# A mixing and scan kernel: preparation by whole chunks, with a third input buffer, a two-bank eviction and another order of the work

## The reference, cut to what matters

```python
# x: (16, 64, 128, 64) float32 = b, h, n, c;   4 heads, channel c = v * 4 + s
xg = group_norm(x)                                   # 32 groups of 2 channels, over h and n
mixed = einsum('mns,bwnvs->bwmvs', softmax(...), xg) # a 128 x 128 matrix for each head s
x = x + mixed + token_bias                           # called x1 below
y = group_norm(x)
row = y[:, 0]
for h in 1..63:  row = y[:, h] + relu(conv1d(row, W))   # 9 taps over n, 64 -> 64 channels
out = x + stack(rows)
```

## Time and profile before

| | |
|---|---|
| median of 3 runs | 876.46 us (875.48 to 876.52) |
| the profiled execution | 875.68 us, span 873.6 us |
| busy PE, DVE, ACT, POOL | 799.9, 618.7, 642.9, 435.7 us |
| preparation alone | from 24.4 to 236.1 us |
| scan with preparation | from 236.1 to 596.6 us |
| end of that wave, scan alone | to 604.0, to 873.6 us |

### The profile page before, as it was taken

How to read it: one execution, slowest core, us unless ns; L and a number is a source line. 1 busy time by engine, 2 the same in 40 slices (tenths; PEclk the granted TensorE clock), 3 DMA queues, 4 the chain that set the end, 5 groups by cost and what they waited for, 6 DMA issues and landing times.

```text
span 873.6 us, 20141 instructions
## 1 busy us (share of the span) xinstructions
PE 799.9 (92%) x5734; PEld 732.1 (84%) x5734; DVE 618.7 (71%) x1536; ACT 642.9 (74%) x1462; POOL 435.7 (50%) x416
## 2 busy tenths in 40 slices
PE   1778887888799999999999999997999999999997
PEld 1555555555599999999899999997999999999997
DVE  7677778777578888989797978765555555555553
ACT  2477777777758887888788888887677677677664
POOL 1665655566265655566566665662333333333333
PEclk9999999999999999999999999999999999999999
DMA  9334343433134444444434343221222222223223
GB/s 186 68 74 96 74 96 72 90 78 83 38 74 93 90 97 98 98 90 94 90 84 91 87 96 74 49 50 37 62 62 67 66 60 67 65 60 68 64 60 72
DMA packets 203159, 68.18 MB, mean 78 GB/s; under 512 B 137556, under 2 KB 203092, under 8 KB 203092
## 3 DMA queue, kind: packets, MB, share of 16 engines
q1 hardware_dynamic: 203092, 67.43, 35.0%
HBM read 33.85 MB, written 33.55 MB: 77 GB/s over the span
## 4 chain that ended last, share of the span: by engine, by line
PE 71%; issue 9%; ACT 7%; DVE 7%; POOL 3%; ACTq 1%; DMA 1%; SPq 1%; DVEq 0%; POOLq 0%
PE ps_conv L898 30%; PE ps_conv L902 15%; PE ps_mix L812 8%; PE ps_mix L814 6%; PE ps_out L890 5%; ACT x_paired L424 5%; PE ps_in L827 5%; PE ps_small L801 2%; POOL xs L341 2%; POOL total L364 1%; DVE carry L732 1%; DVE x_sb L642 1%; DVE st L553 1%; DVE st L649 1%; DMA x_sb<-in_x_dram 1%
## 5 line engine op out<-in xcount | busy, mean ns | idle before, releaser
L364 POOL TENSOR_TENSOR total<-x_paired,carry 128x256 f32<-128x256 f32 x256 | 193.5, 757 | 299.6 <-DVE carry L732 293.5
L341 POOL TENSOR_TENSOR xs<-x_sb,rstd 128x512 f32<-128x512 f32 x128 | 232.9, 1846 | 93.6 <-DVE rstd L624 66.8
L424 ACT ACTIVATE x_paired<-ps_in,shift 64x256 f32 (+1 forms) x512 | 237.9, 465 | 7.8 <-POOL total L364 1.2
L740 DVE TENSOR_TENSOR carry_l<-carry,carry_h 128x256 fp32r<-128x256 f32 x252 | 177.0, 703 | 86.3 <-ACT carry_h L483 83.7
L898 PE MATMUL ps_conv<-carry_h,wh 128*128 128x256 f32 x1280 | 219.7, 303 | 4.7 <-ACT carry_h L483 4.7
L463 ACT ACTIVATE rows<-x_paired,shift,rstd 128x128 f32 (+1 forms) x512 | 221.3, 481 | 0.9 <-DVE shift L672 0.7
L483 ACT ACTIVATE carry_h<-carry 128x256 fp32r<-128x256 f32 x252 | 105.8, 420 | 140.9 <-DVE carry L732 139.0
L898 PE MATMUL ps_conv<-carry_h,wl 128*128 128x256 f32 x1280 | 197.7, 285 | 0.0
L902 PE MATMUL ps_conv<-carry_l,wh 128*128 128x256 f32 x1280 | 196.8, 284 | 0.0
L898 PEld LDWEIGHTS ps_conv<-carry_h,wh 128*128 128x128 f32 x1280 | 176.9, 192 | 7.2 <-ACT carry_h L483 5.6
L898 PEld LDWEIGHTS ps_conv<-carry_h,wl 128*128 128x128 f32 x1280 | 174.0, 190 | 0.0
(11 more groups left out here) (73 smaller groups left out, 354.9 us busy)
## 6 DMA issues: line engine op xcount, KB each, us to landing
x_sb<-in_x_dram SPq DMA_DIRECT2D x64, 512.0 KB, 4.0
out_dram<-staged SPq DMA_DIRECT2D x256, 128.0 KB, 2.4
x_paired<-in_L_conv_W_dram SPq DMA_DIRECT2D x2, 80.0 KB, 2.7
x_paired<-in_L_conv_W_dram SPq DMA_DIRECT2D x2, 64.0 KB, 2.4
x_paired<-v_attention_centers_dram SPq DMA_DIRECT2D x1, 0.0 KB
x_paired<-v_attention_spreads_dram SPq DMA_DIRECT2D x1, 0.0 KB
bias_col<-v_token_proj_n_bias_dram SPq DMA_DIRECT2D x1, 0.5 KB, 5.3
```

The source lines that it names most:

```text
L341: nc.gpsimd.tensor_tensor(xs[:, c % 2, heads, :, :], src, rstd1[:, m:G:2].unsqueeze(1).unsqueeze(1).to_broadcast([P, CG, CR, V]), ALU.mult ...
L364: nc.gpsimd.tensor_tensor(total[s][:, :].rearrange("p (w j) -> p w j", w=WS), x1_rows(wave, it, i, 1, s * WS, WS)[:, 0, :, :], carry[s][:, ...
L424: ins = nc.scalar.activation(dst[q * C:(q + 1) * C, r:HR:2, :], src[:, q, :, :], ACT.Identity, bias=shift1[r * C:(r + 1) * C, e:e + 1])
L740: nc.vector.tensor_tensor(carry_l[s][:, :, EDGE:EDGE + J], carry[s][:, :].rearrange("p (w j) -> p w j", w=WS), carry_h[s][:, :, EDGE:EDGE ...
```

## The change

- There are three input buffers. The third is the memory of `rows`, which the scan needs only later; `buf_of(b)` picks the buffer in the stage alone. Loads run up to three images ahead.
- `ps_mix`, `ps_in` and `ps_conv` are two banks wide. In the stage alone the chunks use `ps_mix` and `ps_conv` in turn. The identity matmuls of L814 and ACT's copy of L432 are gone: one DVE instruction of 128 x 1024 adds the whole chunk, reading the two banks with a stride and x without one.
- `stats1` takes all 64 rows in one instruction: 16 `bn_stats` of 256 columns for an image. The averages need one matmul where they needed two.
- `keep_in` copies a chunk in four instructions of 64 x 512. `norm_rows` works on groups of 4 rows.
- `rstd1` has two buffers. POOL's second-norm power comes later, and the stage alone is written without loops, DVE's list in a new order (`alone_chunk`). In the scan the places of the preparation move: POOL scales one half a step, PE multiplies it after `convolve(t, 0)` and transposes a whole chunk every other step.

The core of the diff, indentation cut by eight columns:

```diff
     HR = CR // 2
-    RG = 2
+    RG = 4
...
+x_bufs = [x_sb[:, 0, :], x_sb[:, 1, :], rows[:, :, :, :, :].rearrange("p a g w j -> p (a g w j)")]
+ps_conv = pb("ps_conv", 2)
+ps_mix = pb("ps_mix", 2)
+ps_in = pb("ps_in", 2)
...
-mean2 = ps_small[:, 66:67]
-var2_ps = ps_small[:, 68:69]
+mean2 = [ps_out[:, 0:1], ps_small[:, 66:67]]
+var2_ps = [ps_out[:, 2:3], ps_small[:, 68:69]]
...
+    for b in range(1, W + 1):
+        for c in range(CH):
+            load_chunk(b, buf_of(b), c, None if b < XB else CH * (b - XB) + c + 1)
+    for c in range(CH - 1):
+        load_chunk(W + 1, 1, c, CH * (W - 1) + c + 1)
...
-    def scale_chunk(b, e, c):
...
+    def scale_half(b, e, k, c, m):
...
+        if m == 0:
+            if c == 0:
+                pool.wait_ge(rstd1_ready, b + 1)
+            if not (isinstance(n, int) and n < 2):
+                pool.wait_ge(mix_done, n - 1)
+        heads = slice(2 * m, 2 * m + 2)
+        src = x_bufs[e][:, c * CC:(c + 1) * CC].rearrange("p (h v s) -> p s h v", v=V, s=S)[:, heads]
+        nc.gpsimd.tensor_tensor(xs[:, c % 2, heads, :, :], src,
+                                rstd1[:, k, m:G:2].unsqueeze(1).unsqueeze(1).to_broadcast([P, CG, CR, V]),
+                                ALU.mult).then_inc(xs_ready, 1)
...
+        if i == 0 and prev:
+            scale_half(b, e, e, 0, 1)
         if i % 2 == 1 and i < STEPS - 1:
-            scale_chunk(b, e, (i + 1) // 2)
-        if i == 6 and prev:
+            scale_half(b, e, e, (i + 1) // 2, 0)
+        if i % 2 == 0 and i > 0:
+            scale_half(b, e, e, i // 2, 1)
+        if i == 5 and prev:
             rstd2_of(b - 1)
         if i == 7 and more:
-            scale_chunk(b + 1, 1 - e, 0)
+            scale_half(b + 1, 1 - e, 1 - e, 0, 0)
...
+    for b in range(W):
+        for c in range(CH):
+            for m in range(2):
+                scale_half(b, buf_of(b), b % 2, c, m)
+            if c == 1 and b > 1:
+                rstd2_of(b - 2)
+    for m in range(2):
+        scale_half(W, 0, 0, 0, m)
+    rstd2_of(W - 2)
...
+        dst = x1_chunk(wave, bw, c)
+        for r, q in ((0, 0), (0, 1), (1, 0), (1, 1))[first:first + count]:
+            src = ps_in[r * C:(r + 1) * C, :].rearrange("p (k j q) -> p q k j", k=HR, q=2)
+            ins = nc.scalar.activation(dst[q * C:(q + 1) * C, r:CR:2, :], src[:, q, :, :],
+                                       ACT.Identity, bias=shift1[r * C:(r + 1) * C, k:k + 1])
+        if first + count == 4:
+            ins.then_inc(in_kept, 1)
...
+        first = 2 * (i % 2)
+        if i < 2 and prev:
+            keep_in(b - 1, 1 - e, 1, it - 1, CH - 1, first, 2, it * STEPS)
+        if i >= 2:
+            keep_in(b, e, 1, it, i // 2 - 1, first, 2, it * STEPS + i // 2 * 2)
...
-                    for k in range(2):
-                        norm_rows(wave, it + g // GROUPS, g % GROUPS, (i % RG) * 2 * NS + 2 * s + k)
+                    norm_rows(wave, it + g // GROUPS, g % GROUPS, (i % RG) * NS + s)
...
+    for w in range(W - 2):
+        first_rows(0, w)
+    keep_in(W - 1, 1, 0, W - 1, CH - 1, 0, 4, None)
+    for w in range(W - 2, W):
+        first_rows(0, w)
...
+    def stats1(b, e, first, count):
+        for c in range(CH):
+            dve.wait_ge(x_loaded[e][c], 16 * (b // XB + 1) if isinstance(b, int) and b <= W else 8 * b - 16 + 8 * e)
+        v = x_bufs[e].rearrange("p (h m g e) -> p m h e g", m=G // 2, g=2, e=CG)
+        for m in range(first, first + count):
+            ins = nc.vector.bn_stats(st1[:, 0, 2 * m:2 * m + 2, :].rearrange("p g k -> p (g k)"),
+                                     v[:, m, :, :, :])
...
+    def rstd1_of(b, k):
-        if not is_zero(b):
-            dve.wait_ge(xs_ready, 2 * CH * b)
-        nc.vector.scalar_tensor_tensor(rstd1[:, :], ratio1[:, :], 1.5, guess1[:, :],
+        if not (isinstance(b, int) and b < 2):
+            dve.wait_ge(xs_ready, 2 * CH * b - 2 * CH)
+        nc.vector.scalar_tensor_tensor(rstd1[:, k, :], ratio1[:, :], 1.5, guess1[:, :],
                                        ALU.add, ALU.mult).then_inc(rstd1_ready, 1)
...
-    def mix_to_x1(b, e, c, m):
-        dve.wait_ge(mix_done[m], b * CH + c + 1)
-        v = x_sb[:, e, c * CC:(c + 1) * CC].rearrange("p (n s) -> p s n", s=S)[:, 2 * m:2 * m + 2, :]
-        nc.vector.scalar_tensor_tensor(v, ps_mix[m][:, :].rearrange("p (s n) -> p s n", s=2),
-                                       bias_col[:, 0:1], v, ALU.add, ALU.add).then_inc(x1_done[m], 1)
+    def mix_to_x1(b, e, c, ps):
+        dve.wait_ge(mix_done, b * CH + c + 1)
+        v = x_bufs[e][:, c * CC:(c + 1) * CC].rearrange("p (n s) -> p n s", s=S)
+        nc.vector.scalar_tensor_tensor(v, ps[:, :].rearrange("p (s n) -> p n s", s=S),
+                                       bias_col[:, 0:1], v, ALU.add, ALU.add).then_inc(x1_done, 1)
...
+        if i % 2 == 1 and gap == 3:
+            mix_to_x1(b, e, i // 2, ps_mix)
...
+            if i in (3, 5) and gap < 3:
+                stats1(b + 1, 1 - e, 10 * (i // 4) + 2 * gap, 2)
+            if i == 4 and gap % 2 == 0:
+                stats1(b + 1, 1 - e, 6 + gap, 2)
+            if i == 6 and gap == 2:
+                dev_of(b + 1)
+                dev2_of(b + 1)
+                m2_of(b + 1)
+            if i == 7 and gap == 0:
+                variance1(b + 1)
+            if i == 7 and gap == 2:
+                guess1_of(b + 1)
+                square1_of(b + 1)
+                ratio1_of(b + 1)
+                rstd1_of(b + 1, 1 - e)
+            if i == 7 and gap == 3:
+                mean_rstd1(b + 1, 1 - e)
...
+    def alone_chunk(b, c):
+        e = buf_of(b)
+        mix_to_x1(b, e, c, (ps_mix, ps_conv)[c % 2])
+        nb, ne, nk = b + 1, buf_of(b + 1), (b + 1) % 2
+        ahead = b + 2 <= W
+        ae = buf_of(b + 2)
+        if c == 0:
+            if b == 0:
+                stats1(nb, ne, 0, 9)
+            stats1(nb, ne, 9, 4)
+            if b > 0:
+                stats2(b - 1, 0, b - 1, 2, 0)
+                stats2(b - 1, 0, b - 1, 2, 1)
+            stats1(nb, ne, 13, 3)
+        if c == 1:
+            dev_of(nb)
+            if b > 0:
+                stats2(b - 1, 0, b - 1, 3, 0)
+            dev2_of(nb)
+            if b > 0:
+                stats2(b - 1, 0, b - 1, 3, 1)
+            m2_of(nb)
+            if b > 0:
+                moments2(b - 1)
+            if b > 1:
+                shift2_of(b - 2)
+        if c == 2:
+            variance1(nb)
+            stats2(b, 0, b, 0, 0)
+            if b > 0:
+                deviations2(b - 1, 0)
+            stats2(b, 0, b, 0, 1)
+            guess1_of(nb)
+            if ahead:
+                stats1(b + 2, ae, 0, 1)
+            square1_of(nb)
+            if ahead:
+                stats1(b + 2, ae, 1, 1)
+            ratio1_of(nb)
+            if ahead:
+                stats1(b + 2, ae, 2, 1)
+            rstd1_of(nb, nk)
+            if ahead:
+                stats1(b + 2, ae, 3, 1)
+        if c == 3:
+            mean_rstd1(nb, nk)
+            if ahead:
+                stats1(b + 2, ae, 4, 3)
+            stats2(b, 0, b, 1, 0)
+            if b > 0:
+                variance2(b - 1, 0)
+            stats2(b, 0, b, 1, 1)
+            keep_shift1(nb, nk)
+            if ahead:
+                stats1(b + 2, ae, 7, 2)
...
+    def mix_half(b, c, m, ps, free):
         n = b * CH + c
         pe.wait_ge(xs_ready, 2 * n + m + 1)
+        if m == 0 and free is not None:
+            pe.wait_ge(x1_done, free)
+        for s in (2 * m, 2 * m + 1):
+            ins = nc.tensor.matmul(ps[:, s * CR * V:(s + 1) * CR * V], mix[:, s, :],
+                                   xs[:, c % 2, s, :, :].rearrange("p h v -> p (h v)"), start=True, stop=True)
+        if m == 1:
+            ins.then_inc(mix_done, 1)
...
-    def mix_bank(b, e, c, m, with_x=False):
...
-        for s in (2 * m, 2 * m + 1):
-            head = ps_mix[m][:, (s % 2) * CR * V:(s % 2 + 1) * CR * V]
-            ins = nc.tensor.matmul(head, mix[:, s, :], xs[:, c % 2, s, :, :].rearrange("p h v -> p (h v)"), start=True, stop=not with_x)
-            if with_x:
-                ins = nc.tensor.matmul(head, ident[:, :], x_sb[:, e, c * CC + s:(c + 1) * CC:S],
-                                       start=False, stop=True)
-        ins.then_inc(mix_done[m], 1)
...
-    def turn_in(b, e, c, u):
+    def turn_in(b, e, c):
         n = b * CH + c
-        for m in range(2):
-            pe.wait_ge(x1_done[m], n + 1)
+        pe.wait_ge(x1_done, n + 1)
         if not is_zero(n):
-            pe.wait_ge(in_kept, 2 * n - 1 + u)
-        for k in range(HR // 2):
...
+            pe.wait_ge(in_kept, n)
+        for k in range(HR):
+            at = c * CC + 2 * k * C
+            ins = nc.tensor.transpose(ps_in[:, k * P:(k + 1) * P], x_bufs[e][:, at:at + P], ident[:, :])
         ins.then_inc(in_turned, 1)
...
+    def prep(b, e, i, after, prev, more):
...
+            mix_half(b, i // 2, i % 2, ps_mix, b * CH + i // 2)
+        else:
```

(29 more changed lines are left out.)

411 lines of the change are left out of this document (168 added, 243 removed).

## The result

The changed kernel takes **891.31 us** (median of 4 runs, 889.9 to 893.26), the kernel before 875.97 us beside it: the ratio is 1.0177 [1.0164, 1.0189], slower by 1.8%. The forecast was 840 us, faster. The profiled execution of the changed kernel has a span of 891.3 us, 17.7 more than before.

A forecast was written before the change was run, and what follows sets the result against it. Preparation alone was taken as bound by a ring of PE and ACT, the two scan stages by PE's own work. 875.7 - 31 (first stage) - 3 (scan with preparation) - 1.7 (end of wave) = 840 us; range 814 to 867.

The forecast's parts named there:

- Scan with preparation: Scan while later images are prepared: two small averages go, a wait for `xs` comes; 3 us gained, bounds 0 to 12.
- The rival on the other side: Wide eviction at 2.2 us fills the scan's odd steps, 4.2 to 4.4 against 3.8 us: 889 us, chance 0.06.
- The three other rivals: Old eviction rate alone, 874 us (0.07); PE's clock falling, 866 (0.08); no hold-ups and a smooth scan, 812 (0.12).
- Eviction: DVE's 128 x 1024 eviction takes 1.21 us, since x's stride of four columns was the slow thing; otherwise 2.2.
- Image in the first stage: Preparation alone, with DVE ending an image: 21.2 us an image against 25.4; wrong if over 23 or under 19.
- first carry: End of preparation alone: the scan's first carry comes at 205 us instead of 236.1, 31 us gained.
- The hold-up: DVE's two-SBUF-operand instructions wait for POOL's scalings, up to one each: 0 to 5.4 us an image, 2.5 taken.
- the small instructions: DVE's list in preparation alone: 16 small instructions, between 0.36 and 0.15 us each, 3.4 us an image.
- `stats1`'s waits: Preparation alone: `stats1` waits for four loads instead of two, in seven places, 0.5 us put down.
- End of the wave: End of wave 0, last eviction inside the last step and fewer keeps by ACT: 1.7 us gained before the aggregate.
- Scan alone: Scan without preparation, bound by PE's own work: nothing gained, unchanged at 4.2 us a step.
- PE's clock: Rival: PE falls to its lower clock in the first stage, 26 us lost, 866 us; chance 0.08.

The follow-up runs named there:

- The first experiment: Changed kernel with PE multiplying a scaled half behind the second convolution of a scan step instead of between the two: 841.67 us, 0.9604.
- the fault put by itself into the kernel before: Kernel before with only the scan's mixing matmuls moved from behind a step's two convolutions to between them: 913.13 us, 1.0431.

## Why the prediction was wrong

**The step that failed** is the term "Scan with preparation": 3 us gained, with 0 to 12 as bounds. It was 56 us lost. It named the right wait, PE's for `xs`, and put it down as "1 to 1.5 us an image, as much as is freed". I compared, at an image's start only, when PE wants the half and when the scaling is done. The comparison holds in every step: POOL's scaling stands behind the second addition, PE's use of it ahead of the second convolution, and the two are joined into a ring by `carry[1]`. The wait can't be seen by adding up anyone's work; POOL has half its time free. The links could have been added from the trace of before: carry 0.42, `total` 0.74, scaling 1.89 (half of a pair's 3.77), mixing 0.73, second convolution 1.83. That is 5.6 us, already PE's own mean of a step (356.2 / 64), before anything is put down for the gaps between them; in the step shown above, with a scaling of 1.95, these bring it to 6.3. The first experiment, and the fault put by itself into the kernel before (+37 us), show it from both sides. Of that stage, moving the mixing takes 51 us (563.9 - 197.9 = 366.0 against 416.9), moving the variance matmul 13 more (550.4 - 197.0 = 353.4). Then it is 7 us *under* before's 360.5, inside the forecast's bounds of 0 to 12: these were right for PE's work and left its waits out.

**A second miss, of the same kind.** `dev2` and `m2`, held up by POOL, were priced for DVE's list alone; in step 6 of the scan PE's `var1_of` waits for their outcome, 1.5 us on average and 7 times. The moved matmul shows 12 us for it.

**No rival held it.** The rival on the other side, at 889 us, gave nearly the measured number, by luck and by a mechanism that wasn't there: it needed an eviction of 2.2 us. The changed kernel with an eviction of 2.08 took 923. The three other rivals ended at 874 or less.

Point by point, the rest:

- Eviction 1.21 forecast, 1.27 measured: right, with its reason. The Trainium skill's note on cachelines (SBUF — State Buffer) says that PSUM access patterns that aren't contiguous slow matmuls down; for DVE's read of the banks no row bears that out. The prediction read only this half of the note. The other half gives SBUF cachelines of 16 bytes and a penalty for each access that crosses to a new line, as each one of x does at a stride of four 4-byte columns; the trace agrees with its 2.08 us against 1.27.
- Image in the first stage 21.2 forecast, 19.7 measured; first carry 205 forecast, 198.75 measured: 37 us gained, not 31. The hold-up was sized right (the square takes 2.3 us on average, 2.5 were put down for all). Too much was counted for the small instructions: in a row each overlaps the next as the long ones do. From 66.0 to 184.3 us DVE's rows sum to 132 us in 118, some 0.05 us for each of 44 instructions an image, and I had left that out for sixteen of them. The 0.5 us for `stats1`'s waits wasn't there either: DVE stood 0.2 us ahead of those rows in the whole stage.
- End of the wave: 4.6 us from the last clearing of `carry_l` to the aggregate, 6.75 before: 2.2 gained, 1.7 forecast. Scan alone: 267.3 us for 64 steps, its step unchanged.
- PE's clock: 0.89 in the first stage after 1.00 before, so this rival was partly there. From 140 to 144 us the granted clock was 0.50, the lower level (1.2 GHz), after PE had waited 2.57 us for the held-up `dev` chain; the eight mixing matmuls from 141.09 on took 3.76 us, and those of 134.16, at 1.00, 1.89. DVE waited 0.57 us for them at 144.89. It cost little, not the 26 us of the rival: from 66.0 to 184.3 us all of DVE's waits for PE add up to 2.2.
- The sum, against the profiled spans: -37.3 (first stage) + 56.4 (scan with preparation) - 2.2 (end of the wave) + 0.8 (from the aggregate on) = +17.7 us.

Open is why a ring closed in every second step, by pairs of scalings, costs three quarters as much as a ring closed in each (38 us against 51), and how the 37 us of the first stage divide among the buffers, ACT's copy, the identity matmuls and the new order: no run takes these apart.

## What to carry to other kernels

When a step of one engine is moved, ask for each thing that it reads behind what its producer issues it, and whether that hangs on something that the moved step now stands ahead of. If so, add the links of the loop, with the gaps between them, and compare them with the busiest engine's own work in that step, not only with its mean; busy shares don't show it, since every engine in such a ring looks underused. Where an input comes from an engine that also serves the recurrence, use what the step before has made, and place the user behind the whole recurrence of its own step.

## What the runs showed of the hardware

- A DVE instruction with two SBUF inputs can be held up through more than one POOL instruction in a row: 32 columns took 3.10 us, to the end of a run of four scalings, and 0.29 on average when placed elsewhere. It went on to the end of the run in six of seven images, and got in between two scalings in one (1.33 us). I had priced one scaling at most. `bn_stats` of 512 columns, with one input, took its 0.68 just ahead of it, while POOL ran. The Trainium skill (SBUF — State Buffer, Who interferes with whom) names the contention, and the trace agrees with its 3.10 us; what these rows add is that DVE mostly doesn't get in between two of POOL's instructions.
- DVE's add of 1024 columns, PSUM and SBUF in: 1.27 us with PSUM at a stride of 256 elements and SBUF contiguous, 2.08 us with PSUM contiguous by head and SBUF at a stride of four. The stride costs on the SBUF side; whether in reading x or in writing it, no run takes apart.
- Shortening one link of a closed ring wins only in part where a second ring stands behind it: half the scaling won 25 us of the kernel's time, moving the user 50.
